# Windowed attention in a fused decoder kernel: 64 key columns for each 32 queries, and value sums on 64x64 tiles

## The reference

```python
def local_attention(q, k, v):            # b, h, n = 128, d = 64
    w = WINDOW; nw = n // w
    bq = q.reshape(b, h, nw, w, d)
    ...
    bk2, bv2 = look(bk), look(bv)        # the window before and the own one: 64 keys
    mask = (it < jb) | (it > jb + w) | (jb == -1)
    sim = jnp.einsum('bhwie,bhwje->bhwij', bq, bk2) * QK_SCALE
    sim = jnp.where(mask, -jnp.finfo(sim.dtype).max, sim)
    attn = jax.nn.softmax(sim, -1)
    out = jnp.einsum('bhwij,bhwje->bhwie', attn, bv2)
    return out.reshape(b, h, n, d)

for i in range(DEPTH):                   # 6
    x = attn_layer(shift_tokens(x), Wqkv[i], q_scale[i], k_scale[i], Wo[i]) + x
    x = ffn_layer(shift_tokens(x), ln_g[i], ln_b[i], W1[i], b1[i], W2[i], b2[i]) + x
```

## Time and profile before

| | |
|---|---|
| median of 3 runs | 4208.51 us |
| the profiled execution | 4210.7 us, its span 4208.9 us, mean granted clock 0.989 |
| busy: PE, DVE, ACT, POOL | 93%, 88%, 84%, 80% of the span |
| steps of the layer loop | 768, in six layers |
| HBM read, written | 21.92 MB, 2.10 MB |

### The profile page before, as it was taken

How to read it: one execution, slowest core, us unless ns; L and a number is a source line. 1 busy time by engine, 2 the same in 40 slices (tenths; PEclk the granted TensorE clock), 3 DMA queues, 4 the chain that set the end, 5 groups by cost and what they waited for, 6 DMA issues and landing times.

```text
span 4208.9 us, 137255 instructions
## 1 busy us (share of the span) xinstructions
PE 3918.9 (93%) x49504; PEld 3102.0 (74%) x49504; DVE 3703.7 (88%) x8896; ACT 3550.0 (84%) x11595; POOL 3379.4 (80%) x2461
## 2 busy tenths in 40 slices
PE   7998885999999999989999999999899999999998
PEld 5666664777777777777777777777777777777776
DVE  7998887999988999979999889999799998899996
ACT  6888995999977999959999779999599997699995
POOL 4554446999978999969999789999599997799993
PEclk9999997999999999999999999999999999999999
DMA  3000000000000000010000000000100000000001
GB/s 84 0 0 1 0 0 16 3 2 0 0 21 22 5 0 0 1 41 4 2 0 0 15 28 5 0 0 1 41 4 2 0 0 13 15 5 0 0 1 36
DMA packets 81122, 38.89 MB, mean 9 GB/s; under 512 B 60084, under 2 KB 73266, under 8 KB 80946
## 3 DMA queue, kind: packets, MB, share of 16 engines
q1 hardware_dynamic: 80946, 36.56, 3.3%
HBM read 21.92 MB, written 2.10 MB: 6 GB/s over the span
## 4 chain that ended last, share of the span: by engine, by line
ACT 42%; PE 33%; DVE 13%; issue 10%; POOL 2%; ACTq 1%; SPq 0%; DMA 0%; DVEq 0%; POOLq 0%
ACT pair L1052 20%; PE bank L771 12%; ACT prob_t L1069 7%; ACT vout L1063 6%; ACT qk_t L1034 5%; PE bank L691 5%; PE pair L848 4%; PE bank L698 3%; DVE top L1443 3%; PE bank L793 2%; DVE qk_parts L1418 2%; PE bank L864 2%; PE bank L672 1%; DVE by_sin L1411 1%; ACT prob L977 1%
## 5 line engine op out<-in xcount | busy, mean ns | idle before, releaser
L1214 POOL TENSOR_TENSOR rnorm<-norm2g,neg_half 128x16 f32<-128x16 f32 x384 | 1115.3, 2905 | 181.7 <-DVE norm2g L1512 172.4
L1052 ACT ACTIVATE pair<-pair,top 128x128 f32<-128x128 f32 x3072 | 1055.8, 345 | 34.9 <-DVE top L1519 24.2
L1206 POOL TENSOR_TENSOR rotated<-by_cos,by_sin 128x512 f32<-128x512 f32 x768 | 985.8, 1284 | 51.0 <-DVE by_sin L1495 44.4
L1226 POOL TENSOR_TENSOR rotated<-rotated,rnorm 128x512 f32<-128x512 f32 x768 | 785.3, 1043 | 0.5
L698 PE MATMUL bank<-wqkv_high,xt_high 128*128 128x512 f32 (+1 forms) x1536 | 649.5, 423 | 15.9 <-ACT squares L1043 14.5
L1052 ACT ACTIVATION_READ_ACCUMULATOR pair<-pair,top 128x1 f32 x3072 | 652.3, 212 | 0.0
L1487 DVE TENSOR_TENSOR by_cos<-bank,rot_cos 128x512 f32<-128x512 f32 x768 | 529.9, 690 | 108.2 <-PE bank L698 91.5
L1063 ACT ACTIVATE vout<-bank 128x512 f32<-128x512 f32 (+1 forms) x810 | 466.0, 575 | 150.5 <-PE bank L771 145.1
L771 PE MATMUL bank<-prob_t,vout 128*32 128x128 f32 x12288 | 495.2, 279 | 94.0 <-ACT prob_t L1069 56.8
L1537 DVE TENSOR_TENSOR prob<-pair,rsum 128x512 f32<-128x512 f32 x768 | 530.9, 691 | 40.0
L1043 ACT ACTIVATE squares<-bank 128x512 f32<-128x512 f32 x768 | 458.8, 597 | 109.7 <-DVE by_sin L1495 92.0
(11 more groups left out here) (142 smaller groups left out, 8451.6 us busy)
## 6 DMA issues: line engine op xcount, KB each, us to landing
wqkv_sb<-in_L_ffn_Wqkv_dram SPq DMA_DIRECT2D x36, 256.0 KB, 4.0
ctx_all<-y SPq DMA_DIRECT2D x48, 128.0 KB
ctx_all<-y SPq DMA_DIRECT2D x48, 127.0 KB
wo_sb<-in_L_ffn_Wo_dram SPq DMA_DIRECT2D x48, 64.0 KB, 2.0
out_dram<-y SPq DMA_DIRECT2D x8, 256.0 KB, 3.5
w_sb<-in_L_ffn_W_dram SPq DMA_DIRECT2D x6, 341.0 KB, 3.0
w_sb<-in_L_ffn_W_dram SPq DMA_DIRECT2D x12, 64.0 KB
cst<-in_constants_dram SPq DMA_DIRECT2D x1, 582.0 KB, 3.9
```

What stands on the lines that cost most here:

```text
L1052: last = nc.scalar.activation(at, at, ACT.Exp, bias=top[jl % 2][:, h:h + 1], accum_out=psum_raw[jl % 2][:, h:h + 1])
L1206: nc.gpsimd.tensor_tensor(rotated[j % 4][:, :, :, :], by_cos[j % 2][:, :, :, :], by_sin[j % 2][:, :, :, :], ALU.add).then_inc(c_rot, 1)
L1214: nc.gpsimd.tensor_tensor(rnorm[slot][:, :, :].rearrange("t g n -> t (g n)"), norm2g[slot][:, :, :].rearrange("t g n -> t (g n)"), neg_hal ...
L1226: nc.gpsimd.tensor_tensor(at, at, rnorm[slot][:, i, :].unsqueeze(2).to_broadcast([P, 2 * HG, DH]), ALU.mult).then_inc(c_unit, 1)
```

## The change

For each 32 queries only 64 key columns are kept: the queries 0 to 63 take keys 0 to 63, queries 64 to 95 take keys 32 to 95, and queries 96 to 127 take keys 64 to 127. A group's scores are then 128 by 4 × 64 instead of 128 by 4 × 128. The probabilities of two heads turn together, with the keys of one head on partitions 0 to 63 and of the other on 64 to 127. The value sums use 64x64 tiles of the array, whose contraction is over 64 partitions; where the values of those keys lie on other partitions, SP moves them with DMAs (`move_values`, four for each two steps). The result of the sums is copied by ACT in a new function, `win_copy_sums`, and `win_project_out` waits for it. The lists of the engines take a new order, `WIN.turn` goes from 3 to 4 and `WIN.exp` from 6 to 5.

```diff
 class WIN:
-    turn = 3
+    turn = 4
     scores = 5
     top = 5
-    exp = 6
+    exp = 5
     scale = 6
     probs = 7
     value = 7
     out = 8
+KEYS = 2 * PAD
+BASES = (0, PAD, 2 * PAD)
...
+            def move_values(l, it, pair):
+                j = 2 * pair + 1
+                sp.wait_ge(c_vout, l * VOUTS + it * STEPS + j + 1)
+                if has(it * STEPS + j - STEPS):
+                    sp.wait_ge(c_value, l * GROUPS + it * STEPS + j - STEPS + 1)
+                elif l:
+                    sp.wait_ge(c_value, l * GROUPS)
+                for i, n, base in ((0, 0, BASES[1]), (0, 1, BASES[2]), (1, 0, BASES[0]), (1, 1, BASES[1])):
+                    sp.dma_start(vmoved[pair][i * KEYS:(i + 1) * KEYS, :, n, :],
+                                 vout_all[base:base + KEYS, 2 * pair:2 * pair + 2, (2 + i) * P:(3 + i) * P]).then_inc(c_moved[pair], 16)
...
             for l in range(DEPTH):
                 if l:
                     shift_tokens(l - 1)
                     sp.wait_ge(c_wo, NB * l)
...
+                if l + 1 < DEPTH:
+                    load_wqkv(l + 1)
+                move_layer(l)
...
             def win_scores(layer, it, j):
                     for i in range(2):
-                        for lower, keys in ((0, slice(0, DH)), (DH, slice(WINDOW, P))):
+                        for lower, n, base in ((0, DH, BASES[0]), (DH, PAD, BASES[1]), (DH + PAD, PAD, BASES[2])):
                             for e in range(2):
-                                last = nc.tensor.matmul(win_ps[jl % 2][lower:lower + DH, e, i * P + keys.start:i * P + keys.stop],
...
+                                last = nc.tensor.matmul(win_ps[jl % 2][lower:lower + n, e, i * KEYS:(i + 1) * KEYS],
+                                                        qk_t[jl % 4][rows, q0:q0 + n], qk_t[jl % 4][rows, k0:k0 + KEYS],
                                                         start=False, stop=False, skip_group_check=True, tile_position=(e * DH, lower))
...
             def win_turn_probs(layer, it, j):
-                    for h in range(HG):
-                        last = nc.tensor.transpose(turn_c_ps[:, h * P:(h + 1) * P], prob[jl % 2][:, h, :], ident)
+                    for e in range(2):
+                        last = nc.tensor.transpose(value_ps[:, e * P:(e + 1) * P], prob[jl % 2][:, e, :], ident)
...
+            def sums_ready(layer, it, j):
+                if here(it, j, WIN.value):
+                    jl = (j - WIN.value) % STEPS
+                    if jl % 2 == 0:
+                        pe.wait_ge(c_moved[jl // 2], 64 * (layer * ENDED + it + (1 if j >= WIN.value else 0)))
+                    if here(it, j, WIN.scale):
+                        pe.wait_ge(c_scaled, layer * GROUPS + it * STEPS + j - WIN.scale + 1)
+                    pe.wait_ge(c_vout, layer * VOUTS + it * STEPS + j + 1)
...
             def win_sum_values(layer, it, j):
-                    for half in range(2):
-                        for h in range(HG):
-                            last = nc.tensor.matmul(value_ps[PAD * h:PAD * (h + 1), half * P:(half + 1) * P],
...
+                    for n, (lower, width) in enumerate(((0, DH), (DH, PAD), (DH + PAD, PAD))):
+                        for e in range(2):
+                            for i in range(2):
+                                last = nc.tensor.matmul(out_ps[e * DH:(e + 1) * DH, lower:lower + width], values_of(j, i, e, n),
+                                                        vout[j][rows, e * P + lower:e * P + lower + width],
+                                                        start=True, stop=True, tile_position=(i * KEYS, e * DH))
...
             def win_heads(layer, it, j):
                     for k in range(4):
+                        if k == 3 and not isinstance(it, int):
+                            sums_ready(layer, it, j)
...
             def win_project_out(layer, it, j):
+                    pe.wait_ge(c_sum, m + 1)
...
             def win_products(layer, it, j):
                 win_project(layer, it, j)
                 win_turn_probs(layer, it, j)
                 win_values(layer, it, j)
+                win_project_out(layer, it, j)
+                win_heads(layer, it, j)
                 win_mask(layer, it, j)
                 win_scores(layer, it, j)
                 win_sum_values(layer, it, j)
-                win_heads(layer, it, j)
-                win_project_out(layer, it, j)
...
             def win_copies(layer, it, j):
-                win_exponentials(layer, it, j)
-                win_copy_probs(layer, it, j)
-                win_square(layer, it, j)
                 win_copy_values(layer, it, j)
                 win_copy_heads(layer, it, j)
+                win_square(layer, it, j)
+                win_exponentials(layer, it, j)
+                win_copy_sums(layer, it, j)
...
             def win_step(layer, it, j):
+                win_recip(layer, it, j)
+                win_scale(layer, it, j)
                 win_cos(layer, it, j)
                 win_sin(layer, it, j)
-                win_recip(layer, it, j)
-                win_scale(layer, it, j)
                 win_max(layer, it, j)
```

More of the change, by code:

```diff
@@ L131, in constants @@
     put("causal", np.where(ahead >= 0, 0.0, MASKED))
-    band = np.where((ahead >= 0) & (ahead <= WINDOW), 0.0, MASKED)
-    put("band", np.concatenate([np.tile(band[lower:lower + DH], (2, 1)) for lower in (0, DH)], 1))
+    band = np.where((ahead >= 0) & (ahead <= WINDOW), 0.0, MASKED)[0:DH, 0:KEYS]
+    put("band", np.concatenate([np.tile(b, (2, 1)) for b in (band, np.tile(band[WINDOW:DH], (2, 1)))], 1))
     return t
@@ L379, in build @@
         c_value = sem("c_value")
+        c_sum = sem("c_sum_copied")
+        c_moved = [sem(f"c_values_moved{i}") for i in range(STEPS // 2)]
         c_wo = sem("c_wo_done")
@@ L446, in ended, with last_sum @@
             return isinstance(it, int) and it >= ENDED
-        def turned_ps(it):
-            return proj_ps if ended(it) else heads_ps
+        def last_sum(it, j):
+            return ended(it) and j == WIN.value - 1
         def opening(b):
@@ L683, in win_heads @@
                     pe.wait_ge(c_unit, g + 1)
-                    if ended(it) and j == 0:
-                        pe.wait_ge(c_sq, (layer + 1) * GROUPS)
-                    if has(it * STEPS + j - WIN.turn - 1) and (ended(it) or not here(it, j, WIN.probs)):
+                    if has(it * STEPS + j - WIN.turn - 1):
                         pe.wait_ge(c_qk, g)
@@ L760, in win_sum_values @@
             def win_sum_values(layer, it, j):
                 if here(it, j, WIN.value):
-                    m = layer * GROUPS + it * STEPS + j - WIN.value
-                    jl = (j - WIN.value) % STEPS
-                    if not here(it, j, 0):
-                        pe.wait_ge(c_vout, layer * VOUTS + it * STEPS + j)
-                    pe.wait_ge(c_pt, m + 1)
-                    for half in range(2):
-                        for h in range(HG):
-                            at = 2 * P + h * DH + half * PAD
-                            last = nc.tensor.matmul(value_ps[PAD * h:PAD * (h + 1), half * P:(half + 1) * P],
-                                                    vout[jl][:, at:at + PAD], prob_t[jl % 2][:, h % 2 * 2 + h // 2, :],
-                                                    start=True, stop=True, tile_position=(0, PAD * h))
+                    if isinstance(it, int):
+                        sums_ready(layer, it, j)
@@ L790, in win_project_out @@
                         pe.wait_ge(c_xsplit, layer * NB + xt_before(b))
[L791 to L793 removed]
+                    pe.wait_ge(c_sum, m + 1)
+                    for i in range(2):
+                        k = 2 * (jl % NG) + i
+                        last = nc.tensor.matmul(acc_ps[:, 0:P], prob_t[(j - 1) % 2][:, i, :], wo_sb[:, k * P:(k + 1) * P],
                                                 start=(k == 0), stop=(k == 2 * NG - 1))
@@ L886, in drain @@
                     win_turn_probs(layer, ENDED, j)
+                    win_heads(layer, ENDED, j)
+                    win_project_out(layer, ENDED, j)
                     win_mask(layer, ENDED, j)
```

115 lines of the change are left out of this document (67 added, 48 removed).

## The result

The change makes the kernel slower by 11%: 4670.86 us median of four runs (4670.22 to 4676.01) against 4208.93 us (4206.87 to 4213.31) before; the ratio is 1.1099, with a 95% interval of 1.1079 to 1.1118. The forecast was 4475 us, with a range from 4185 to 4590. The sign was right, the loss is 462 us instead of 266, and the time lies above the range.

A forecast was written before the change was run, and what follows sets the result against it. A closed loop through PE, DVE and ACT was taken to bound the step at 4.17 us; with the fourth steps +253 us, drain +13, on a 4208.9 us span, plus 1.8 around it, less 2: 4475 us, range 4185 to 4590.

The forecast's parts named there:

- The new loop: Attention step: scores, maximum, exponentials, sums' copy, project_out, heads and mask close a loop once a step, 4.17 us against 3.957.
- The changes of shape: PE, scores and ahead of the sums: each change between 64x64 and 64x32 tiles costs 0.09 us, bounds 0 and 0.09.
- Each fourth step: New sequence's step: late xt_high copy delays DVE's reciprocal and scaling, so PE waits at the fourth heads transpose, 0.52 us.
- Drain and DMA: Layer end: longer drain steps add 13 us; value moves cost nothing; shifts queued behind them 0 to 3 us a layer.
- longer steps in the drain: Layer ends: the same loop without heads behind the wait, 3.73 us a step against 3.2, +13 us over six layers.
- free shape changes within 64 rows: Rival inside win_scores: changes between tiles of 64 rows cost nothing, another loop of 3.72 us takes over, 4195 us; chance 0.20.
- POOL alone: Rival: changes free and fourth step hidden, GpSimd's work bounds the step at 3.70 us, 4020 us; chance 0.04.
- Late values: Rival: each value-move DMA holds SP 2.3 us rather than 0.65, 4.6 us a step, 4680 us; chance 0.06.
- The waits on PE cost more: Listed rival: five semaphore waits among the heads add 0.15 us a step, 4586 us, upper end of forecast's own range.

The follow-up runs named there:

- grouped: Changed kernel with the same score matmuls reordered, all 64x64 tiles first, then the 64x32 tiles, one shape change within the scores instead of three: 4470.67 us.
- input_early: Changed kernel with the next sequence's input turned behind the heads' transposes and copied ahead of the exponentials in every fourth step: 4605.77 us.
- shift_first: Changed kernel with the shifted copies for the layer's end issued ahead of the last value moves in SyncE's queue: 4633.34 us.
- uniform64: Changed kernel with the second half's scores as one 64x64 tile, eight score matmuls instead of twelve, leaving part of the computation out: 4297.68 us.
- no_moves: Changed kernel without the value moves between partitions, so some key windows meet other values, leaving work out: 4632.05 us.
- project_last: Changed kernel with project_out moved to the end of TensorE's step, its wait for the sums' copy going to the fourth heads transpose: 4687.70 us.
- heads_first: Changed kernel with project_out and its wait for the sums' copy moved behind the third of four heads transposes: 4503.84 us.

## Why the prediction was wrong

The sign and the mechanism of the plain step, a new loop closed once a step, were right. It fell 196 us short, by three terms: the size of the plain step (122 us), the fourth step, where the wait itself was the wrong one (56 us), and the layer ends, where the time for a copy to land was (28 us). That makes 206; the first and last steps of a layer lengthen less than those between them, which takes back 12 and leaves the 194 us that lie between the forecast and the profiled spans (460 less 266).

**The new loop, 4.17 us a step.** The mechanism was right and the size low by 0.165 us, × 738 = 122 us, the largest part. Link by link from PE's records, of which these, cut to a few hundredths of a microsecond, are the first of `project_out` and of the heads:

```profile
2254.12 0.38 PE L842 MATMUL bank<-wo_sb,prob_t 128*128 128x128 f32 x1 [0.18 <-ACT prob_t L1123]
2254.66 0.27 PE L727 MATMUL bank<-cst,rotated 128*128 128x128 f32 x1
```

| from the last score matmul's start | forecast | measured |
|---|---|---|
| to the next `project_out` | 2.31 | 2.36 |
| `project_out` to the first heads transpose | 0.49 | 0.55 |
| heads to the masks | 0.53 | 0.53 |
| masks to the scores | 0.08 | 0.08 |
| scores, first to last start | 0.76 | 0.82 |

No link is far out: the hand-over from PE to DVE is 0.07 and not 0.04, ACT's four exponentials 1.17, and at `project_out`, after the wait, the second record comes 0.21 behind the first and not 0.11, where the forecast had added 0.05. The 0.06 of the scores lies mostly in tiles that start 0.007 apart after a change, 0.02 in each set of four, which the forecast had at nothing. In a loop closed once a step each such 0.05 us costs 37 us. The changes of shape, the term that the forecast called most doubtful, were right at 0.09: the row for 128x128 to 128x64 in the earlier trace rows held for 64x64 to 64x32 as well. (The Trainium skill, page "TensorEngine Tiling (Array Packing)", section Key Properties, says that changing the tiling mode drains the engine. The runs agree that this change costs time, 0.27 us for two of them in grouped; the draining itself no run here shows.)

**Each fourth step, 0.52 us.** This is the step of the forecast whose reasoning failed. The forecast let the late `xt_high` copy delay reciprocal and scaling, and PE wait for them at the fourth heads transpose. The trace shows PE stopped before that, at `project_out`, for the addition to `y` (`c_yadd`), which stands behind the split. The wait for the sums' copy had been counted at `project_out`, and the two others written in the same function, for `c_yadd` and `c_xsplit` at the first group of a sequence, had not. Split, addition and a hand-over of 0.21 us (2263.45 to 2263.66) all lie on the path: 0.88 us in the step shown. Over eight steps it is less, since the second fourth step has 5.05 us: eight `by_cos` intervals take 36.33 us, the forecast had 34.40, and of the 1.93 between them the plain steps account for 1.32. The 0.61 left, × 92.25, is 56 us. input_early took the wait away and brought the step to 4.71.

**Drain and DMA, 0 to 3 us a layer taken as 0.** The queue's order had been seen, its size missed: 7 us a layer. The forecast gave the shifts some 2 us to land, from no row of theirs; the 127-row copy took 9 us from its issue, and DVE waited 7.50. The trace of before already had this, 8.8 us (2371.89 to 2380.69), but there the copy stood behind nothing. The forecast's 13 us for longer steps in the drain came for another reason than it gave: with the shifts first the layer ends take 81.0 us, no more than the 81.3 before, so the drain's steps cost nothing and the queue all of the 41. Against the 13 that is 28 us short. shift_first recovered 38.

The rivals: free shape changes within 64 rows (4195 us) are refuted by grouped and uniform64. POOL alone (4020) is refuted by POOL's 387.56 busy of 472.70 us. Late values (4680) would have given nearly the time that was measured, for a wrong reason: no_moves refutes them. "The waits on PE cost more", at 0.15 us a step, comes nearest in the plain steps, 0.165, though the excess sits in refills, tile starts and a hand-over and not among the semaphores of the heads (0.53 forecast and measured). What the forecast's own range left out was that this, the fourth step and the drain could all be short at once: all three erred to one side. No run put the exponentials back one step behind the maximum with the narrow keys, which would have opened the loop by itself; the loop is shown by its chain and by the runs that shortened it (grouped) or took it off the chain (project_last, heads_first).

## What to carry to other kernels

When a wait is moved onto an in-order engine, list every wait in that function with the work queued behind each partner, and not just the one the change is about; and price each refill in a closed loop by a measured one, since 0.05 us a step was 37 us here. The work of an engine, laid end to end from the trace, should be compared with the old step before anything else: PE's 4.0 to 4.1 us against 3.957 said slower with no wait at all. And a slower kernel may be a good idea in a poor order: the same arithmetic, with tiles of one shape run together and the late item off the critical place, went from 11% slower to 0.7% faster.

## What the runs showed that was not expected

- Four edits that each remove a wait or a gap added up almost exactly (470 singly, 466 together), although they act on one loop.
- A change of tile shape from 64x64 to 64x32 costs 0.135 us in all at the same number of rows, 0.09 of it between the last record and the first. The two changes that another order saves were a quarter of the scores' time (1.03 to 0.76 us).
- Moves of 64 KB between partitions, 1152 + 384 of them, were free beside the loop (the queue's share of the DMA engines' time is 12.0% with them and 3.0% without). A copy of 127 rows in pieces of 256 bytes was another matter: 9 us from issue to its last piece, where the 128-row copy beside it moved its pieces in about 1, and whatever was issued behind it was held for 6.39 to 6.82 us.
